# Loading part of the token rows later, and moving one copy of a query piece to another queue, in a fused cross-attention and mixture-of-experts layer

## The reference

```
x = x + tanh(g_xattn) * xattn(layernorm(x), ctx, mask, Wq, Wkv)
    q = layernorm(x) @ Wq.T;  k, v = ctx @ Wkv.T;  softmax(where(mask, q k / 4, -1e9)) @ v
x = x + tanh(g_ffn) * ffn(layernorm(x))
    two best of 8 experts: silu(h @ fc1_a) * (h @ fc1_b) @ fc2, weighted, plus a shared expert
```

## Time and profile before

| what | value |
|---|---|
| median of 3 runs | 325.39 us (325.25 to 326.46) |
| the profiled execution's own time | 323.84 us |
| its span in the profile | 322.1 us |
| TensorE busy | 303.1 us (94% of the span) |
| VectorE busy | 242.4 us (75%) |
| ScalarE busy | 169.2 us (53%) |
| GpSimd busy | 131.8 us (41%) |
| TensorE clock granted | full throughout |

### The profile page before, as it was taken

How to read it: one execution, slowest core, us unless ns; L and a number is a source line. 1 busy time by engine, 2 the same in 40 slices (tenths; PEclk the granted TensorE clock), 3 DMA queues, 4 the chain that set the end, 5 groups by cost and what they waited for, 6 DMA issues and landing times.

```text
span 322.1 us, 8146 instructions
## 1 busy us (share of the span) xinstructions
PE 303.1 (94%) x2535; PEld 243.8 (76%) x2535; DVE 242.4 (75%) x728; ACT 169.2 (53%) x322; POOL 131.8 (41%) x153
## 2 busy tenths in 40 slices
PE   8976999999989988999999999899999999999996
PEld 8764768787768755655585878678888888888885
DVE  4487689798999998688799996456666666644697
ACT  2535677787777754357693534434444444424240
POOL 5761233241466745415771049943333443331000
PEclk9999999999999999999999999999999999999999
DMA  7976567586665462167256122233333333202943
GB/s 210 304 173 174 188 187 243 162 256 192 192 180 162 143 179 87 37 195 280 83 171 134 43 59 78 75 106 98 108 95 99 94 91 101 73 21 77 429 147 130
DMA packets 33877, 47.18 MB, mean 146 GB/s; under 512 B 5519, under 2 KB 27411, under 8 KB 33330
## 3 DMA queue, kind: packets, MB, share of 16 engines
q1 hardware_dynamic: 28272, 34.34, 35.8%
q0 software_dynamic: 4416, 11.18, 10.6%
q10 hardware_dynamic: 1154, 1.18, 1.3%
HBM read 22.20 MB, written 12.62 MB: 108 GB/s over the span
## 4 chain that ended last, share of the span: by engine, by line
PE 54%; issue 16%; POOL 11%; DVE 10%; DMA 5%; ACT 1%; SPq 1%; DVEq 0%; POOLq 0%; ACTq 0%
PE ps L1805 32%; POOL dispatched L549 4%; PE ps L1627 4%; DVE mx L999 2%; DMA expert_rows<-v_s,slot_u 2%; PE ps L1853 2%; PE ps L1776 2%; PE ps L1797 2%; PE ps L1638 2%; DMA x_all<-in_x 2%; POOL work L559 2%; POOL rs L534 2%; PE ps L1487 1%; DMA stacks<-work 1%; POOL stacks L568 1%
## 5 line engine op out<-in xcount | busy, mean ns | idle before, releaser
L614 POOL DMA_INDIRECT expert_rows<-v_s,slot_u x39 | 38.3, 983 | 72.7 <-ACT v_s L894 44.1
L999 DVE TENSOR_REDUCE mx<-ps 128x8 f32<-128x1024 f32 x32 | 39.1, 1223 | 11.1 <-PE ps L1487 10.9
L559 POOL TENSOR_TENSOR work<-work 128x512 bf16<-128x512 f32 x16 | 18.5, 1155 | 46.7 <-ACT work L665 46.6
L696 ACT ACTIVATE probs<-ps 128x1024 f32<-128x1024 f32 x32 | 32.7, 1022 | 8.9 <-PE ps L1520 8.8
L1320 DVE TENSOR_TENSOR act<-ps,sil 128x256 f32<-128x256 f32 x39 | 16.6, 425 | 26.6 <-ACT sil L887 26.6
L887 ACT ACTIVATE sil<-ps 128x256 f32<-128x256 f32 x39 | 15.0, 384 | 41.1 <-PE ps L1805 41.1
L1805 PE MATMUL ps<-fc_hi,xs_hi 128*128 x78 | 34.3, 440 | 0.0
L1805 PE MATMUL ps<-fc_hi,xs_lo 128*128 x78 | 30.7, 394 | 0.0
L1805 PE MATMUL ps<-fc_lo,xs_hi 128*128 x78 | 30.7, 394 | 0.0
L894 ACT ACTIVATE v_s<-ps,wt 128x256 f32<-128x256 f32 x39 | 18.5, 474 | 22.3 <-PE ps L1805 22.3
L1805 PE MATMUL ps<-fc_hi,act_hi 128*128 x78 | 22.4, 287 | 2.6 <-DVE act_lo L1331 2.5
(11 more groups left out here) (222 smaller groups left out, 823.6 us busy)
## 6 DMA issues: line engine op xcount, KB each, us to landing
stacks<-work SPq DMA_DIRECT2D x73, 128.0 KB, 2.9
xs_in<-dispatched SPq DMA_DIRECT2D x39, 129.0 KB, 2.1
fc_s<-in_fc SPq DMA_DIRECT2D x8, 512.0 KB, 4.3
stacks<-work POOLq DMA_DIRECT2D x20, 128.0 KB, 3.5
ctx_s<-in_ctx_t SPq DMA_DIRECT2D x8, 256.0 KB, 4.0
fc_s<-in_fc SPq DMA_DIRECT2D x8, 256.0 KB, 4.8
stacks<-expert_rows SPq DMA_DIRECT2D x2, 1024.0 KB, 6.0
probs<-expert_rows SPq DMA_DIRECT2D x2, 1024.0 KB, 10.7
```

The source lines that it names most:

```text
L559: nc.gpsimd.tensor_tensor(out[:, 2, :], rest, out[:, 1, :], ALU.subtract).then_inc(ready, 1)
L614: nc.gpsimd.indirect_dma_start(ys, bass.IndirectOffsetOnAxis(dst_u[:, r:r + 1], 0), y_out[:, r, :], None, bounds_check=2 * T - 1, oob_is_e ...
L696: nc.scalar.activation(probs[:, 2 * j + h], ps_t, ACT.Exp, scale=HD ** -0.5).then_inc(probs_ok[j][h], 1)
L999: nc.vector.reduce_max(mx[:, j, 8 * h:8 * h + 8], ps_s, AX_X).then_inc(max_ok[j][h], 1)
```

## The change

The last load of rows is split: blocks 4 to 9 (`MIDDLE` = 10) come where all twelve came, and blocks 10 to 15 are loaded by SyncE after the copies of group 0, with a semaphore of their own (`x_last`). SyncE also issues the copy of the first group's third query piece (`stack_q(0, 2)`), which GpSimd issued before; the third key piece stays with GpSimd. The waits on `q3_in` go, and `copied` counts this copy on the query semaphore.

On VectorE, `stats` and `first_norm` of the third batch cover six blocks. For the late six, four `bn_stats` stand at the end of step 2, the other two with the six `bn_aggr` and the addition after the maxima's pieces of step 3, and `first_norm` at the same place of step 4. GpSimd's `power1` for them stands in step 3 after `power2(0, 1)`. `norm1` waits for the fourth batch from group 5 on.

```diff
         def copied(taken, g):
             whole = 96 + 48 * (g // 2) if taken is kst else 96 * (g // 2 + 1)
-            return whole if g % 2 else whole - 16
+            return whole if g % 2 or taken is qst else whole - 16
...
-            sp.dma_start(x_all[:, 4:B, :], x_view[:, 4:B, :]).then_inc(x_rest, 16)
+            sp.dma_start(x_all[:, 4:MIDDLE, :], x_view[:, 4:MIDDLE, :]).then_inc(x_rest, 16)
             stack_k(0, 0)
             stack_k(0, 1)
             stack_q(0, 1)
+            stack_q(0, 2)
+            sp.dma_start(x_all[:, MIDDLE:B, :], x_view[:, MIDDLE:B, :]).then_inc(x_last, 16)
...
             third(0, kst, k_rest, k_ok[1], k_pc, k_ok[2])
-            third_of_first(k_ok[2], k_st, k_pc, K_ROWS[5][1], khi[0])
+            third_of_first_keys()
             third(0, qst, q_rest, q_ok[1], q_pc, q_ok[2])
-            third_of_first(q_ok[2], q_st, q_pc, Q_ROWS[5][1], q3_in)
-            power1(4, B, 3)
+            power1(4, MIDDLE, 3)
...
                 if live(s - 3):
                     power2(s - 3, 1)
+                if s == 3:
+                    power1(MIDDLE, B, 4)
...
-                sa.wait_ge(nm_ok, min(g + 1, 3))
+                sa.wait_ge(nm_ok, min(g + 1, 3) + (2 * g >= MIDDLE))
...
-            def stats(b0, b1):
+            def half_stats(b0, b1):
                 for b in range(b0, b1):
                     nc.vector.bn_stats(st1[:, b, :], x_all[:, b, :]).then_inc(dve_link, 1)
                 links[0] += b1 - b0
+
+            def stats(b0, b1, first=None):
+                half_stats(b0 if first is None else first, b1)
                 ve.wait_ge(dve_link, links[0])
...
             ve.wait_ge(x_rest, 16)
-            stats(4, B)
+            stats(4, MIDDLE)
             rest(1, ps_kq, k_ok[0], k_pc, k_ok[2], k_rest, kr_ok)
             maxima(0, 0, 0)
-            first_norm(4, B, 3)
+            first_norm(4, MIDDLE, 3)
...
                     pieces(s - 2, 1)
+                if s == 2:
+                    ve.wait_ge(x_last, 16)
+                    half_stats(MIDDLE, B - 2)
+                elif s == 3:
+                    stats(MIDDLE, B, B - 2)
+                elif s == 4:
+                    first_norm(MIDDLE, B, 4)
```

More of the change, by code:

```diff
@@ L257, in build_program @@
         sums = [ps[:, 4 + t, 0:D] for t in range(CH)]
-        names = """x_in0 x_in1 x_rest ctx_in0 ctx_in1 wq_in wk_in wv_in kones_ok small_in wr_in ffn_in down_in fc1_in fc2_in fc1_late fc2_late
+        names = """x_in0 x_in1 x_rest x_last ctx_in0 ctx_in1 wq_in wk_in wv_in kones_ok small_in wr_in ffn_in down_in fc1_in fc2_in fc1_late fc2_late
             const_ok tanh_ok gates_done zero_row_ok v_ones_ok wr_ok
             ln1_var rs1_ok nm_ok xn_ok xnt_done xnt_ok k_done q_done v_done v_ok
-            k1_ok k2_ok k3_ok q1_ok q2_ok q3_ok kr_ok qr_ok qst0 qst1 kst0 kst1 khi0 khi1 q3_in
+            k1_ok k2_ok k3_ok q1_ok q2_ok q3_ok kr_ok qr_ok qst0 qst1 kst0 kst1 khi0 khi1
             s_done00 s_done01 s_done10 s_done11 max_ok00 max_ok01 max_ok10 max_ok11 pieces_ok0 pieces_ok1
@@ L280, in two @@
             return [S[f"{name}{j}"] for j in range(2)]
-        x_in0, x_in1, x_rest = S["x_in0"], S["x_in1"], S["x_rest"]
+        x_in0, x_in1, x_rest, x_last = S["x_in0"], S["x_in1"], S["x_rest"], S["x_last"]
         wq_in, wk_in, wv_in, kones_ok = S["wq_in"], S["wk_in"], S["wv_in"], S["kones_ok"]
@@ L293, in build_program @@
         ctx_in, qst, kst, rows_in, scat = two("ctx_in"), two("qst"), two("kst"), two("rows_in"), two("scat")
-        khi, q3_in = two("khi"), S["q3_in"]
+        khi = two("khi")
         s_done, max_ok, st_done, probs_ok, pv_done = (four("s_done"), four("max_ok"), four("st_done"),
@@ L323, in held @@
             return value if isinstance(value, int) else eng.to_reg(value)
+        MIDDLE = 10
         BANKS_0 = (5, 6)
@@ L352, in copied, with keys_by_pool @@
             whole = 96 + 48 * (g // 2) if taken is kst else 96 * (g // 2 + 1)
-            return whole if g % 2 else whole - 16
[L355 to L359, removed]
+            return whole if g % 2 or taken is qst else whole - 16
+        def keys_by_pool(g):
+            return 16 * (g % 2 == 0) + 48 * (g // 2)
         @block.sync
@@ L556, in third @@
                     pool.wait_ge(taken[(g - 1) % 2], copied(taken, g - 1))
-                if g == 1:
-                    pool.wait_ge(khi[0] if taken is kst else q3_in, 16)
+                if g == 1 and taken is kst:
+                    pool.wait_ge(khi[0], 16)
                 nc.gpsimd.tensor_tensor(out[:, 2, :], rest, out[:, 1, :], ALU.subtract).then_inc(ready, 1)
@@ L569, in stack_k_high, with third_of_first_keys @@
                                             k_pc[:, p, :]).then_inc(khi[g % 2], 16)
[L571 to L574, removed]
+            def third_of_first_keys():
+                pool.wait_ge(k_ok[2], 1)
+                nc.gpsimd.dma_start(k_st[K_ROWS[5][1]:PIECES * HD:PIECES, 0].rearrange("p h t -> p (h t)"),
+                                    k_pc[:, 2, :]).then_inc(khi[0], 16)
             power1(0, 2, 1)
@@ L656, in first @@
                     sa.wait_ge(taken[(g - 1) % 2], copied(taken, g - 1))
[L657 to L660, removed]
+                if g and taken is kst and keys_by_pool(g - 1):
+                    sa.wait_ge(khi[(g - 1) % 2], keys_by_pool(g - 1))
                 nc.scalar.activation(out[:, 0, :], whole, ACT.Copy).then_inc(ready, 1)
@@ L1474, in scores @@
                     pe.wait_ge(kst[g % 2], copied(kst, g))
[L1475 to L1478, removed]
+                    if keys_by_pool(g):
+                        pe.wait_ge(khi[g % 2], keys_by_pool(g))
                     if g:
```

## The result

The changed kernel takes 323.75 us in the median of 5 runs (322.95 to 323.99); the kernel before takes 325.39 us (324.65 to 326.46). The ratio is 0.994, interval [0.9911, 0.9968]: faster by 1.6 us, three times the forecast of 0.5. The profiled execution took 323.62 us, span 321.8.

What follows compares the result with a forecast made beforehand. TensorE, busy 94% at full clock, was the bound, so only its waits counted. -0.5 us at the start, +0.2 at 48 to 51 us and -0.2 from ScalarE's bound gave -0.5: 324.9 us, range 323.7 to 326.4.

Steps and rivals of the forecast that it cites:

- the forecast of 0.5: Whole kernel: the change was to save 0.5 us, from 325.39 to 324.9 us on the median's scale.
- Nothing waits for that (above): zero: Start, VectorE: six statistics instead of twelve end at 16.8 instead of 20.78 us, but this releases nothing, gain zero.
- rival 2: More comes back: full 0.66, ScalarE's 0.42, no late statistics, VectorE's unexplained 0.46; -1.54 us, 323.8 or less; chance 0.13.
- the late statistics: VectorE, 48 to 51 us: 1.4 us of moved work against 1.14 idle, 0.26 late; cost 0.2 us, bounds 0 and 0.3.
- The query copy: Start: SyncE's copy of the third query piece lands 1.2 us earlier, first scores gain 0.35 to 0.66, middle 0.5 us.
- the sign that I had given for being wrong: Start, TensorE: first scores still released by a DMA would show the forecast wrong.
- the 0.5 us: Start, TensorE: first scores earlier by 0.5 us, the middle of 0.35 to 0.66, through SyncE's query copy.
- fit of 2.3 us: Start: the skill page's estimate for GpSimd's 128 KB copy, landing near 20.0; the prediction used the measured 4.44 us instead.
- The second load was harmless: Issued on SyncE at about 18.1, it delays the next key copies by a microsecond at most; cost zero.
- VectorE's idle before them: Before the maxima at 34.69, four statistics of 1.34 us hide in 2.39 us of idling, leaving 1.05.
- Rival 1: Nothing arrives: the second load shares DMA engines with GpSimd's key copy and delays the queries; 325.3 to 325.6 us; chance 0.20.
- ScalarE's issues: Start: issuing three query copies takes ScalarE 2.34 us against SyncE's 1.92; up to 0.42 us more, about half counted.

Runs made afterwards that it cites:

- the pair with the same fill: 20 warming matmuls before the second block's first scores, in the changed kernel and in the kernel before: ratios 0.9967 and 1.0015, medians 324.62 and 325.72 us.
- the two filled ones: Kernel before with warming matmuls added in four gaps (ratio 1.0055), and with 20 in the one gap before the second block's first scores (1.0015).
- statistics_only: Kernel before with statistics and power of blocks 10 to 15 moved as in the change, one load, GpSimd copying the query piece: ratio 0.9987.
- split_only: Kernel before with only the load split and the statistics moved; GpSimd still copies the third query piece: ratio 1.0049.
- split_issue_later: Kernel before with load split and statistics moved, GpSimd copying the query piece, SyncE waiting for that piece before issuing the second load: ratio 1.0088.
- again_after: Changed kernel, unaltered, measured again against the kernel before: ratio 0.9956, median 324.70 us; profiled execution 326.21 us.
- third_after: Changed kernel, unaltered, measured a third time against the kernel before: ratio 0.9979, median 323.97 us.

## Why the prediction was right in sign and wrong in size

**The size.** At full clock the medians are 324.63 (39 executions) and 323.77 (18): 0.86 us. Over all they are 325.42 and 323.89. So about 0.9 us are shorter waits; the pair with the same fill has 0.85 as well. I put the other 0.7 down to the clock, which stays full in 62% of the executions instead of 24%. This second part is a difference of medians and not an experiment of its own (by the means, 0.75 of 1.05 us are there at full clock).

**The step that failed** is "Nothing waits for that (above): zero", on the halved load and its statistics. It rested on one trace, in which VectorE's subtraction at 20.99 was ready exactly with ScalarE, so halving freed nothing. The trace was right about the order and unlucky as a sample: GpSimd's key copy took 4.8 us in it, and up to 6.4 in other traces with the same front load. Behind it wait the queries and GpSimd's next subtraction, and beside that VectorE's small multiplication. From the first to the third maxima it is 5.3 to 5.9 us in the four traces whose start is that of the kernel before (the two unchanged ones and the two filled ones), and 4.87, 4.88 and 4.89 in those of the changed kernel: 0.5 to 1.0 us less, in place of zero. Of this 0.42 are VectorE's gap. It goes with the moved statistics and not with the load, as statistics_only shows, and its cause stays open; I had it in rival 2 as unexplained. The rest goes with the lighter front: with both loads in front the trace has 5.49 although the gap is gone, while split_only and split_issue_later, with half in front, have 4.89.

From the memset to the third maxima the two traces of the kernel before take 17.7 us both, the three of the changed kernel 16.7 to 17.0. With the 0.28 that the late statistics cost, that is 0.4 to 0.7 us; the full-clock medians say 0.86.

**The query copy: a part of the forecast came, its signs did not.** I took 1.2 us sooner by SyncE's median of 3.4 us. Issued at 18.18 in the first trace and waited for until 22.6, the copy took about 4.4 us, as on GpSimd, and the sign that I had given for being wrong, first scores released by a DMA, is there in two of three traces (0.81 and 0.67 us). The first scores come 11.74 and 11.25 us after the memset before, 11.45, 11.18 and 11.28 after. With the variants that do not touch the start the means are 11.6 (three traces) and 11.0 (six, 10.0 to 11.7). So the 0.5 us may well be there, but the traces of one start spread wider than that. Alone the copy gained nothing in time. What the pair adds to it, the second load kept behind it, is argued above.

**The page on GpSimd's transfers.** By the Trainium skill's fit of 2.3 us ("DMA: Bandwidth & Descriptors", section "Anatomy of one DMA — SWDGE (gpsimd) path") the query copy would not have been a wait. The traces have GpSimd's key copy at 3.4 to 6.4 us from issue to use, the longer ones with the full load in front. The page's account of queues taking turns (section "Queues, rings and completion order") agrees with split_only, where TensorE still waits 1.96 us for GpSimd's copy, in a queue of its own, beside the second load.

**The late statistics** came as worked out: 1.40 us for 1.4, maxima 0.28 late for 0.26, transposes held by 0.2. The second load was harmless for the maxima at 34.69, as said. VectorE's idle before them fell to 1.10 us for 1.05.

**Rival 1** did not come: with the second load behind it the key copy takes 3.4 to 4.8 us, against 4.7 to 6.4 before. **Rival 2** had nearly the right time, and one of its terms came in full, VectorE's gap. ScalarE's issues took 2.04 us in the first trace instead of 2.34, but 2.00 in the second trace of the kernel before, so that is no gain shown; and the late statistics, which it left out, were paid. It lacked the key copy and the clock. I wrote "full clock" from the earlier trace rows of an execution that belonged to the quarter that has it.

**Open:** what VectorE waits for in its gap, why the clock falls in one execution and not in another with the same idle stretch, why half-clock stretches also come in stages where TensorE is busy most of the time, and where split_issue_later loses its time.

## What to carry to other kernels

One trace is one draw. Where timed runs spread by more than the expected gain, first ask whether the profiled execution lies inside them, and look at the mean clock of each run; a second trace of the kernel before showed 5.81 us for 5.34 from the first to the third maxima. The slower key copy came only with further traces, and the missing clock with the clocks of the timed runs. A wait that "hides exactly" under another is not covered, since either can be longer next time. And before a stage full of small dependent steps on TensorE, count its idle time: here the waits that went were worth 0.9 us, and a part of the other 0.7 came with the clock. Filling the idle time with matmuls nobody reads kept the clock, and cost as much as it brought.

## What the runs showed of the hardware

- From issue to use, a 128 KB copy of another queue took 3.4 to 4.8 us with a load of 0.8 MB in front, and 4.7 to 6.4 with 1.5 MB.
- A copy of 12 KB was used 6.0 us after its issue behind 768 KB and six copies of 128 KB in its own queue, TensorE waiting 3.6 of them; without the 768 KB it was 2.6.
- Behind a stretch in which TensorE was busy 1.1 to 1.2 of 2.50 us the granted clock was 0.53 for 6.8 us in one execution (again_after) and 1.00 in another (third_after). With 20 small matmuls in a gap of that stretch: 11 of 12 executions at full clock, against 18 of 29; with 36 fewer before it: 2 of 12.
- Beside a GpSimd subtraction a VectorE multiplication of 12 columns took 0.75 us and one of 6 columns 0.87; the one of 6 columns took 0.15 with GpSimd idle.
